# Attention and feed-forward kernel: query tiles 2 and 3 turned by VectorE and moved by DMA instead of turned by TensorE

## The chip, the core and the metric

The kernel runs on 1 of the cores of one Trainium2 chip. The metric is the time of one execution on the device in microseconds (us). Engines: TensorE (PE, matmuls), VectorE (DVE), ScalarE (ACT), GpSimd (POOL), and SyncE (SP), which here only issues DMA transfers.

## The reference

The input x has 4 batches of 1024 tokens of 128 numbers, all float32. Attention with 16 heads of 64 comes first, then a layer norm, a small feed-forward part and a second layer norm:

```python
s = einsum('bhid,bhjd->bhij', q * 64**-0.5, k)
gm = max(s, axis=-1, keepdims=True)            # over all columns, masked or not
p = where(triu(ones, 1), 0.0, exp(s - gm))     # causal
out = einsum('bhij,bhjd->bhid', p, v) / (sum(p, -1) + 1e-8)
x = layernorm(x + out @ Wo + bo)
r = sigmoid(mix(x, mu_r) @ W_r.T); k = square(relu(mix(x, mu_k) @ W_k.T))
x = layernorm(x + r * (k @ W_v.T))             # mix: mu * x + (1 - mu) * the token before
```

## The kernel before

Two heads are worked on at a time: a pair. There are 8 pairs in each of 4 batches, so 32 pairs (p) one after the other, and the feed-forward part follows behind them. The 1024 queries of a pair are 8 tiles of 128; one step (t) of a pair makes the scores of tile t for both heads (a = 0, 1). The program of each engine is written out as a loop over p and t, so the order on each engine is the order in the code; semaphores tie the engines together.

One tile goes this way. TensorE writes 128x1024 scores into one of 3 score buffers (`ps_s`, line 758). VectorE moves them, scaled and with their running minimum, into one of 4 slots of `tile` in SBUF (`evacuate`, line 585); a slot comes free two steps later, when its tile is turned. GpSimd masks the 128x128 block on the diagonal (line 340), ScalarE takes the exp of the (t+1)*128 columns that count and sums them (line 434). The values matmul needs this probability tile with keys on the partitions, so it is turned, into `pt`:

- Tiles 0 to 3 are turned on TensorE (`turn_tile`, line 771: one 128x128 transpose for each block of keys, t+1 of them for each head), into one of the 2 shared banks `ps_x`, and ScalarE copies them to `pt` (`take_turned`, lines 472 and 479). They are turned one step later than their scores.
- Tiles 4 to 7 are turned in 32x32 blocks by VectorE (line 596) into a staging buffer. When both tiles of a unit (unit u is tiles 2u and 2u+1) are turned, SyncE moves the blocks to their partitions with 16 transfers (`move`, line 290), each from 32 partitions to 32 partitions. There are 32 such transfers a pair.

The values matmuls (`values`, line 808) come in three parts: part 0 (units 0 and 1) in step 7 of the same pair, part 1 (unit 2) in step 5 of the next pair, part 2 (unit 3) in step 6 of the next pair. What they give goes through ScalarE (`take_values`, line 457) to `ot`, is scaled by 1/sum on GpSimd (`norm`, line 347, with `rb`, which two DMA transfers from ScalarE's queue spread), is projected by TensorE (`project_out`, line 819, half 0 in step 4), and is added to `y`. Between these stand the projections of the next pair: three matmuls for each half of q and k (line 694, steps 0 to 3), which ScalarE takes and GpSimd splits into a high and a low part, and the value projections (line 703, steps 0 and 1).

The two shared banks `ps_x` go round in the order of their users (`users_of_banks`); a user waits until the one before it in its bank has been copied out (`drained`).

## Time and profile before

| | |
|---|---|
| time, median of 3 runs | 1148.97 us (1145.62 to 1149.92) |
| profiled execution: time, span | 1145.66 us, 1143.9 us |
| TensorE busy | 1042.7 us, 91% |
| VectorE busy | 924.4 us, 81% |
| ScalarE busy | 735.7 us, 64% |
| GpSimd busy | 565.8 us, 49% |
| mean granted TensorE clock | 0.982 of full |
| transfers stage to pt | 1024 issues, all on SyncE's queue |

Times are of one profiled execution. A matmul row of the timeline merges neighbours of one form, so its start is what to read, not its length: the next row starts when TensorE goes on. Busy shares are means over the whole span; what ends a wait is read from the timeline.

### The profile page before, as it was taken

What the parts mean: (1) busy time and instruction counts of PE and PEld (TensorE: products, weight loads), DVE (VectorE), ACT (ScalarE), POOL (GpSimd) and SP (SyncE); (2) the same over time, 40 slices, a digit from 0 to 9 for tenths busy, and PEclk for the clock granted to TensorE, in tenths of its full rate; (3) what the DMA queues carried; (4) which work ended last, traced back from release to release, by engine and by line L of the source; (5) the groups of instructions that cost most, each with busy time, mean ns of one, the idle gap of its engine ahead of it and who ended that gap; (6) DMA issues with size and microseconds to landing.
All of it is one profiled execution on the core that took longest, in us unless ns stands there. A gap on an engine that the chain in (4) does not pass through costs nothing.

```text
span 1143.9 us, 21976 instructions
## 1 busy us (share of the span) xinstructions
PE 1042.7 (91%) x7411; PEld 675.9 (59%) x7411; DVE 924.4 (81%) x1588; ACT 735.7 (64%) x1666; POOL 565.8 (49%) x904
## 2 busy tenths in 40 slices
...
GB/s 154 82 131 125 129 129 146 149 135 126 120 111 128 133 139 148 143 119 117 129 125 125 134 148 148 126 127 114 125 125 131 144 148 141 120 114 136 83 38 37
DMA packets 172497, 142.44 MB, mean 125 GB/s; under 512 B 26849, under 2 KB 167905, under 8 KB 172385
## 3 DMA queue, kind: packets, MB, share of 16 engines
...
q14 instruction: 54, 0.43, 0.1%
...
## 4 chain that ended last, share of the span: by engine, by line
PE 45%; DVE 23%; issue 12%; POOL 10%; DMA 5%; ACT 2%; SPq 2%; ACTq 1%; DVEq 0%; POOLq 0%
PE ps_s L758 18%; PE ps_x L808 17%; DVE tile L585 12%; DVE stage L596 6%; POOL ot L347 4%; DMA rb<-recips 4%; PE ps_x L819 4%; POOL tile L340 2%; POOL qs L334 2%; PE ps_x L694 2%; PE ps_x L771 2%; SPq L290 2%; PE ps_x L703 1%; POOL qs L332 1%; DVE stats L611 1%
## 5 line engine op out<-in xcount | busy, mean ns | idle before, releaser
L585 DVE TENSOR_SCALAR_CACHE_REDUCE tile<-ps_s 128x1024 f32<-128x1024 f32 x512 | 604.5, 1217 | 175.3 <-PE ps_s L758 173.9
L434 ACT ACTIVATE tile<-tile,neg_max 128x640 f32<-128x640 f32 (+7 forms) x512 | 394.3, 773 | 178.9 <-POOL tile L340 175.2
L758 PE MATMUL ps_s<-ks,qs 64*128 64x512 f32 x3072 | 426.0, 409 | 9.1 <-DVE tile L585 7.0
L340 POOL TENSOR_SCALAR_AFFINE_SELECT tile<-tile 128x128 f32<-128x128 f32 x512 | 148.2, 292 | 426.2 <-DVE tile L585 424.6
L758 PEld LDWEIGHTS ps_s<-ks,qs 64*128 64x128 f32 x3072 | 270.2, 185 | 116.1 <-DVE tile L585 39.3
L808 PE MATMUL ps_x<-pt,vs 128*64 128x256 f32 (+1 forms) x2560 | 270.4, 362 | 2.8 <-DMA pt<-stage 2.8
L596 DVE STREAM_TRANSPOSE stage<-tile 128x640 f32<-128x640 f32 (+3 forms) x256 | 249.7, 1014 | 0.0
L808 PEld LDWEIGHTS ps_x<-pt,vs 128*64 128x64 f32 x2560 | 173.6, 137 | 111.2 <-issue 37.7
L694 PE MATMUL ps_x<-xs,ws 128*128 128x512 f32 x381 | 121.7, 428 | 15.2 <-ACT vs L447 14.5
L347 POOL TENSOR_TENSOR ot<-ot,rb 128x512 f32<-128x512 f32 x64 | 99.2, 1550 | 66.3 <-ACT ot L457 56.1
L771 PE MATMUL ps_x<-ident,tile 128*128 128x128 f32 x640 | 113.8, 284 | 11.9 <-ACT tile L434 10.4
L771 PEld LDWEIGHTS ps_x<-ident,tile 128*128 128x128 f32 x640 | 69.8, 140 | 83.8 <-issue 58.0
L479 ACT ACTIVATE pt<-ps_x 128x256 f32<-128x256 f32 (+2 forms) x192 | 90.6, 489 | 31.7 <-PE ps_x L771 29.0
L441 ACT ACTIVATE x1t<-ps_x 128x512 f32<-128x512 f32 x124 | 74.5, 600 | 55.8 <-PE ps_x L694 34.5
L434 ACT ACTIVATION_READ_ACCUMULATOR tile<-tile,neg_max 128x1 f32 x512 | 97.2, 190 | 0.0
L819 PE MATMUL ps_x<-ot,wos 128*128 128x512 f32 x128 | 73.0, 652 | 25.6 <-POOL ot L347 25.6
L354 POOL TENSOR_TENSOR y<-y,ot 128x512 f32<-128x512 f32 x64 | 82.9, 1295 | 7.1 <-ACT ot L462 7.1
L694 PEld LDWEIGHTS ps_x<-xs,ws 128*128 128x128 f32 x381 | 62.8, 191 | 34.1 <-ACT vs L447 21.9
L334 POOL TENSOR_TENSOR qs<-x1t,qs 128x512 fp32r<-128x512 f32 x62 | 79.5, 1282 | 5.3
L334 POOL TENSOR_TENSOR ks<-x1t,ks 128x512 fp32r<-128x512 f32 x62 | 78.9, 1273 | 5.1
L462 ACT ACTIVATE ot<-ps_x 128x512 f32<-128x512 f32 x64 | 38.2, 597 | 48.3 <-PE ps_x L819 48.3
L703 PEld LDWEIGHTS ps_x<-ws,xs 128*128 128x128 f32 x384 | 49.8, 188 | 28.7 <-ACT ot L457 16.2
...
## 6 DMA issues: line engine op xcount, KB each, us to landing
pt<-stage SPq DMA_DIRECT2D x512, 128.0 KB, 4.6
pt<-stage SPq DMA_DIRECT2D x512, 96.0 KB, 2.2
...
```

Of the source, the lines that this page charges most:

```text
L334: pool.tensor_tensor(lo, full[n % 2], hi.bitcast(F32), ALU.subtract).then_inc(s_qklo, 1)
L340: pool.affine_select(out=block_of, in_=block_of, compare_op=ALU.is_ge, fill=fill, base=0, pattern=[[-1, P]], channel_multiplier=1).then_in ...
L347: pool.tensor_tensor(cols, cols, rb[:, :].rearrange("p (i t) -> p t i", t=TILES)[:, 4 * c:4 * c + 4, :], ALU.mult).then_inc(s_norm, 1)
L434: act.activation(cols, cols, ACT.Exp, bias=neg_max[:, at:at + 1], scale=-1.0, accum_out=sums[:, p % 2, a, t:t + 1]).then_inc(s_exp, 1)
L479: act.activation(place, cols, ACT.Copy).then_inc(s_pt, 1)
L585: dve.tensor_scalar(tile[:, at, :], ps_s[scores_at(p, t, a)][:, :], -SCALE, None, ALU.mult, ALU.min, accum_out=neg_max[:, at:at + 1]).then ...
L596: dve.transpose(stage_unit(u)[:, 2 * a + t % 2, :, 0:32 * (t + 1)], tile[:, slot_of(p, t, a), 0:(t + 1) * P].rearrange("p (j b k) -> p b j ...
L694: ins = mm(bank, ws[:, "qk".index(what), wh, r * P:(r + 1) * P], xs[:, b % XSLOTS, xh, c * HALF:(c + 1) * HALF], start=(m == 0), stop=(m = ...
L758: ins = mm(ps_s[scores_at(p, t, a)][:, c * HALF:(c + 1) * HALF], qs[rows, p % 2, qh, t * P:(t + 1) * P], ks[rows, p % 2, kh, c * HALF:(c + ...
L771: ins = turn(ps_x[BANK[unit]][:, at:at + P], tile[:, slot_of(p, t, a), j * P:(j + 1) * P], ident[:, :])
L808: ins = mm(bank[a * DH:(a + 1) * DH, cols + second * P:cols + 2 * P], vs[:, p // 2 % 2, j, p % 2, a * DH:(a + 1) * DH], moving, start=(j = ...
L819: mm(ps_x[BANK[unit]][:, :], wos[:, p % PAIRS, :], ot[:, c * HALF:(c + 1) * HALF], start=True, stop=True).then_inc(s_out, 1)
```

## The change

Tiles 2 and 3 go the way of tiles 4 to 7. `BLOCKWISE` is now tiles 2 to 7; TensorE turns tiles 0 and 1 only. There are three units to move, 48 transfers a pair, in the order unit 3 of the pair before, unit 1, unit 2. `pt` and the staging buffers have a new layout, in which the two tiles of a unit and both heads lie side by side without gaps, so that each transfer has 32 runs (one for each partition, of 448, 704 or 960 numbers for units 1, 2, 3) where it had 128 (of 192 or 256 numbers). The memsets of the gaps are gone. Unit 1 is read by the values matmuls of the same pair, in step 7.

The orders change too: on VectorE the second turn of tile 7 stands behind the first evacuation of step 1; on TensorE and ScalarE the turned tile comes ahead of the value projection in step 1; ScalarE takes out half 0 in step 5, not 4. The value tiles 4 to 7 have one place instead of two. Two more buffers for the halves of q and k keep ScalarE and GpSimd apart.

```diff
--- before.py
+++ after.py
@@ -27,14 +27,16 @@
 UNITS = TILES // 2
-UNIT_COLS = [(2 * u + 2) * 32 for u in range(UNITS)]
-UNIT_AT = [16 * sum(UNIT_COLS[:u]) for u in range(UNITS)]
+HEAD_COLS = [(4 * u + 3) * 32 for u in range(UNITS)]
+UNIT_COLS = [2 * cols for cols in HEAD_COLS]
+UNIT_AT = [4 * sum(UNIT_COLS[:u]) for u in range(UNITS)]
+PT_COLS = 4 * sum(UNIT_COLS)
 MOVED = 16 * 16
-BLOCKWISE = range(TILES // 2, TILES)
-
-TURNED_IN = {0: ((0, 1),), 1: ((0, 1),), 2: ((0,), (1,)), 3: ((0,), (1,))}
-COPIES = {(0, 0): 1, (1, 0): 3, (2, 0): 4, (2, 1): 5, (3, 0): 6, (3, 1): 7}
-ALL_COPIES = 7
+BLOCKWISE = range(2, TILES)
+
+TURNED_IN = {0: ((0, 1),), 1: ((0, 1),)}
+COPIES = {(0, 0): 1, (1, 0): 3}
+ALL_COPIES = 3
@@ -43,7 +45,7 @@
 V_AT = {0: 0, 1: 1}
-TURN_AT = {1: 0, 2: 1, 3: 2, 4: 3}
+TURN_AT = {1: 0, 2: 1}
 X_AT = 1
@@ -58,6 +60,10 @@
     return 2 * ((TILES * p + t) % (RING // 2)) + a
+
+
+def v_place(i, j):
+    return i % 2 * 4 + j if j < 4 else 4 + j
...
@@ -129,19 +135,20 @@
         ks = sb("ks", [P, 2, 2, N], F32R)
-        vs = sb("vs", [P, 2, TILES, 2, P])
+        vs = sb("vs", [P, TILES + 4, 2, P])
         tile = sb("tile", [P, RING, N])
         recips = sb("recips_sb", [P, 2, 2, TILES])
-        stage = [sb(f"stage{n}", [P, 16 * UNIT_COLS[2 + n]]) for n in range(2)]
-        pt = sb("pt", [P, 16 * sum(UNIT_COLS)])
+        stage = [sb(f"stage{n}", [P, 4 * UNIT_COLS[1 + n]]) for n in range(3)]
+        pt = sb("pt", [P, PT_COLS])
         ot = sb("ot", [P, N])
         x1t = sb("x1t", [P, 1 + N])
-        full = [x1t[:, 1:1 + HALF], x1t[:, 1 + HALF:1 + N]]
+        full2 = sb("full2", [P, HALF])
+        full = [x1t[:, 1:1 + HALF], x1t[:, 1 + HALF:1 + N], full2[:, :], x1t[:, 1:1 + HALF]]
         bo_col = sb("bo_col", [P, 1])
@@ -160,14 +167,18 @@
         def stage_unit(u):
-            return stage[u - 2][:, :].rearrange("p (x b c) -> p x b c", x=4, b=4)
+            return stage[u - 1][:, :].rearrange("p (b c) -> p b c", b=4)
         def pt_unit(u):
-            return pt[:, UNIT_AT[u]:UNIT_AT[u] + 16 * UNIT_COLS[u]].rearrange("p (x a c) -> p x a c", x=4, a=4)
-
-
-
-        idle = pt[:, UNIT_AT[3]:UNIT_AT[3] + 4 * N]
+            return pt[:, UNIT_AT[u]:UNIT_AT[u] + 4 * UNIT_COLS[u]].rearrange("p (a c) -> p a c", a=4)
+
+        def place_of(t, a):
+            at = a * HEAD_COLS[t // 2] + t % 2 * 32 * t
+            return slice(at, at + 32 * (t + 1))
+
+
+
+        idle = pt[:, PT_COLS - 4 * N:PT_COLS]
         x_raw = [idle[:, 0:N]] + [y[:, b * N:(b + 1) * N] for b in range(1, B)]
...
@@ -278,21 +288,23 @@
                 if p == 0 and u == 2:
-                    sp.wait_ge(s_gaps, 2)
                     sp.wait_ge(f_wt, 1)
                 at_least(sp, s_pv, 3 * (p - 1) + u)
-                sp.wait_ge(s_turned, 8 * p + 4 * (u - 2) + 4)
+                sp.wait_ge(s_turned, 12 * p + 4 * u)
                 for a in range(4):
                     for b in range(4):
-                        sp.dma_start(pt_unit(u)[32 * b:32 * b + 32, :, a, :], stage_unit(u)[32 * a:32 * a + 32, :, b, :]
-                                     ).then_inc(s_moved[u - 2], 16)
-
-            for p in range(ALL_PAIRS):
-                move(p, 2)
-                move(p, 3)
+                        sp.dma_start(pt_unit(u)[32 * b:32 * b + 32, a, :], stage_unit(u)[32 * a:32 * a + 32, b, :]
+                                     ).then_inc(s_moved[u - 1], 16)
+
+            for p in range(ALL_PAIRS + 1):
+                if p > 0:
+                    move(p - 1, 3)
+                if p < ALL_PAIRS:
+                    move(p, 1)
+                    move(p, 2)
@@ -310,10 +322,6 @@
-            for n in range(2):
-                pool.memset(stage[n][:, :], 0.0).then_inc(s_gaps, 1)
-
-
             pool.wait_ge(s_wraw, 48)
@@ -329,9 +337,9 @@
                 pool.wait_ge(s_full, done + 1)
-                pool.tensor_copy(hi, full[n % 2]).then_inc(s_qkhi, 1)
+                pool.tensor_copy(hi, full[n]).then_inc(s_qkhi, 1)
                 pool.wait_ge(s_qkhi, done + 1)
-                pool.tensor_tensor(lo, full[n % 2], hi.bitcast(F32), ALU.subtract).then_inc(s_qklo, 1)
+                pool.tensor_tensor(lo, full[n], hi.bitcast(F32), ALU.subtract).then_inc(s_qklo, 1)
@@ -437,14 +445,16 @@
                 act.wait_ge(s_proj, done + 1)
-                at_least(act, s_qklo, done - 1)
-                act.activation(full[n % 2], ps_x[BANK["qk", p, n]][:, :], ACT.Copy).then_inc(s_full, 1)
+
+                at_least(act, s_qklo, done - {0: 0, 1: 3, 2: 3, 3: 2}[n])
+                act.activation(full[n], ps_x[BANK["qk", p, n]][:, :], ACT.Copy).then_inc(s_full, 1)
-                at_least(act, s_pv, 6 * (i - 1))
-                act.activation(vs[:, i % 2, 2 * n:2 * n + 2, :, :],
+                at_least(act, s_pv, 6 * (i - 1) if n < 2 else 6 * i)
+                at = v_place(i, 2 * n)
+                act.activation(vs[:, at:at + 2, :, :],
                                ps_x[BANK["v", i, n]][:, :].rearrange("p (t e c) -> p t e c", t=2, e=2), ACT.Copy
...
@@ -500,26 +510,27 @@
                         take_out(p - 2, 1)
+                    if t in TURN_AT and p < ALL_PAIRS:
+                        take_turned(p, TURN_AT[t], 0)
                     if t in V_AT and p < ALL_PAIRS:
                         take_v(p // 2, 2 * (p % 2) + V_AT[t])
-                    if t in TURN_AT and p < ALL_PAIRS:
-                        take_turned(p, TURN_AT[t], 0)
                     if t in QK_AT and p + 1 < ALL_PAIRS:
                         take_qk(p + 1, QK_AT[t])
-                    if t == OUT0_AT and 0 < p:
+                    if t == OUT0_AT + 1 and 0 < p:
                         take_out(p - 1, 0)
-                    if t in TURN_AT and p < ALL_PAIRS and len(TURNED_IN[TURN_AT[t]]) > 1:
-                        take_turned(p, TURN_AT[t], 1)
                     if t == X_AT and p < ALL_PAIRS:
                             take_x(b, c)
+                    if t == 1 and p > 0:
+                        spread_recips(p - 1)
                     if p < ALL_PAIRS:
                         exp_of(p, t, 0)
+                    if t in TURN_AT and p < ALL_PAIRS and len(TURNED_IN[TURN_AT[t]]) > 1:
+                        take_turned(p, TURN_AT[t], 1)
+                    if p < ALL_PAIRS:
                         exp_of(p, t, 1)
                         column_recips(p - 1)
-                    if t == 1 and p > 0:
-                        spread_recips(p - 1)
                     if t == 5 and p > 0:
@@ -577,9 +588,9 @@
                 if u in BLOCKWISE:
-                    at_least(dve, s_turned, 8 * q + 2 * (u - 4) + a + 1)
+                    at_least(dve, s_turned, 12 * q + 2 * (u - 2) + a + 1)
                 else:
-                    dve.wait_ge(s_quad, 8 * q + 2 * u + a + 1)
+                    dve.wait_ge(s_quad, 4 * q + 2 * u + a + 1)
                 dve.wait_ge(s_scores, SLOTS * p + 2 * t + a + 1)
@@ -589,11 +600,9 @@
-                    at_least(dve, s_moved[u - 2], MOVED * p)
-                if p == 0 and t == 4 and a == 0:
-                    dve.wait_ge(s_gaps, 2)
+                    at_least(dve, s_moved[u - 1], MOVED * p)
                 dve.wait_ge(s_exp, SLOTS * p + 2 * t + a + 1)
-                dve.transpose(stage_unit(u)[:, 2 * a + t % 2, :, 0:32 * (t + 1)],
+                dve.transpose(stage_unit(u)[:, :, place_of(t, a)],
                               tile[:, slot_of(p, t, a), 0:(t + 1) * P].rearrange("p (j b k) -> p b j k", b=4, k=32)
@@ -637,6 +646,9 @@
                         evacuate(p, t, 0)
+                    if t == 1 and p > 0:
+                        turn_tile(p - 1, TILES - 1, 1)
+                    if p < ALL_PAIRS:
                         evacuate(p, t, 1)
@@ -646,7 +658,8 @@
                         turn_tile(q, u, 0)
-                        turn_tile(q, u, 1)
+                        if u < TILES - 1:
+                            turn_tile(q, u, 1)
                     if p == ALL_PAIRS and t == SUMS_AT:
@@ -795,18 +808,22 @@
                     pe.wait_ge(s_pt, ALL_COPIES * (p + 1))
-                else:
-                    pe.wait_ge(s_moved[k - 1], MOVED * (p + 1))
                 for u in units:
+                    if u > 0:
+                        pe.wait_ge(s_moved[u - 1], MOVED * (p + 1))
                     cols = (u % 2) * 2 * P
                     for j in range(final + 1):
-
-                        second = j == final
                         for a in range(2):
-                            moving = pt_unit(u)[:, 2 * a + second:2 * a + 2, :, 32 * j:32 * j + 32]
-                            ins = mm(bank[a * DH:(a + 1) * DH, cols + second * P:cols + 2 * P],
-                                     vs[:, p // 2 % 2, j, p % 2, a * DH:(a + 1) * DH], moving,
+                            at = a * HEAD_COLS[u]
+                            if j < final:
+                                both = pt_unit(u)[:, :, at:at + 2 * 32 * final].rearrange("p a (t c) -> p t a c", t=2)
+                                moving = both[:, :, :, 32 * j:32 * j + 32]
+                            else:
+
+                                moving = pt_unit(u)[:, :, at + 32 * (final + j):at + 32 * (final + j) + 32]
+                            ins = mm(bank[a * DH:(a + 1) * DH, cols + (j == final) * P:cols + 2 * P],
+                                     vs[:, v_place(p // 2, j), p % 2, a * DH:(a + 1) * DH], moving,
                                      start=(j == 0), stop=(j == final))
@@ -839,16 +856,16 @@
                         project_out(p - 2, 1)
+                    if t in TURN_AT and p < ALL_PAIRS:
+                        turn_tile(p, TURN_AT[t], 0)
                     if t in V_AT and p < ALL_PAIRS:
                         v_of(p // 2, 2 * (p % 2) + V_AT[t])
-                    if t in TURN_AT and p < ALL_PAIRS:
-                        turn_tile(p, TURN_AT[t], 0)
                     if t in QK_AT and p + 1 < ALL_PAIRS:
                         qk_of(p + 1, QK_AT[t])
+                    if t in TURN_AT and p < ALL_PAIRS and len(TURNED_IN[TURN_AT[t]]) > 1:
+                        turn_tile(p, TURN_AT[t], 1)
                     if t == OUT0_AT and 0 < p:
                         project_out(p - 1, 0)
-                    if t in TURN_AT and p < ALL_PAIRS and len(TURNED_IN[TURN_AT[t]]) > 1:
-                        turn_tile(p, TURN_AT[t], 1)
                     if t == X_AT and p < ALL_PAIRS:
```

VectorE, from the evacuations of step 7 of one pair to those of step 5 of the next, as it was (`[waits ...]` names semaphores; 128x4x160 is a turned tile of 640 columns, 128x4x224 one of 896):

```order
L585 TENSOR_SCALAR tile,neg_max<-ps_s 128x1024 [waits s_scores,s_turned] x2
L602 TENSOR_SCALAR sums_eps<-sums 128x16 [waits s_exp]
L606 RECIPROCAL recips_sb<-sums_eps 128x16 [waits s_eps,s_rdram]
L596 STREAM_TRANSPOSE stage<-tile 128x1024 [waits s_exp] x2
L585 TENSOR_SCALAR tile,neg_max<-ps_s 128x1024 [waits s_scores,s_turned] x2
L585 TENSOR_SCALAR tile,neg_max<-ps_s 128x1024 [waits s_scores,s_quad] x8
L596 STREAM_TRANSPOSE stage<-tile 128x4x160 [waits s_exp,s_moved0]
L596 STREAM_TRANSPOSE stage<-tile 128x4x160 [waits s_exp]
L585 TENSOR_SCALAR tile,neg_max<-ps_s 128x1024 [waits s_scores,s_turned] x2
```

And as it is now (128x4x96 is tile 2 with 384 columns, 128x4x128 tile 3 with 512):

```order
L596 TENSOR_SCALAR tile,neg_max<-ps_s 128x1024 [waits s_scores,s_turned] x2
L611 TENSOR_SCALAR sums_eps<-sums 128x16 [waits s_exp]
L615 RECIPROCAL recips_sb<-sums_eps 128x16 [waits s_eps,s_rdram]
L605 STREAM_TRANSPOSE stage<-tile 128x4x256 [waits s_exp]
L596 TENSOR_SCALAR tile,neg_max<-ps_s 128x1024 [waits s_scores,s_turned]
L605 STREAM_TRANSPOSE stage<-tile 128x4x256 [waits s_exp]
L596 TENSOR_SCALAR tile,neg_max<-ps_s 128x1024 [waits s_scores,s_turned]
L596 TENSOR_SCALAR tile,neg_max<-ps_s 128x1024 [waits s_scores,s_quad] x4
L605 STREAM_TRANSPOSE stage<-tile 128x4x96 [waits s_exp,s_moved0]
L605 STREAM_TRANSPOSE stage<-tile 128x4x96 [waits s_exp]
L596 TENSOR_SCALAR tile,neg_max<-ps_s 128x1024 [waits s_scores,s_turned] x2
L605 STREAM_TRANSPOSE stage<-tile 128x4x128 [waits s_exp] x2
```

Four turned tiles stand where there were none, two behind the evacuations of step 3 and two behind those of step 4, and the second turn of tile 7 stands between the two evacuations of step 1.

TensorE, steps 3 and 4 behind the scores of step 3, before (L771 is a transpose, L694 a projection of q or k, L819 the projection of the output, L758 the scores):

```order
L771 MATMUL ps_x<-ident,tile 128x128 [waits s_exp,s_pt]
L771 MATMUL ps_x<-ident,tile 128x128 x2
L694 MATMUL ps_x<-xs,ws 128x512 [waits s_full]
L694 MATMUL ps_x<-xs,ws 128x512 x2
L771 MATMUL ps_x<-ident,tile 128x128 [waits s_exp,s_pt]
L771 MATMUL ps_x<-ident,tile 128x128 x2
L758 MATMUL ps_s<-ks,qs 128x512 [waits s_evac]
L758 MATMUL ps_s<-ks,qs 128x512 x11
L771 MATMUL ps_x<-ident,tile 128x128 [waits s_exp,s_full]
L771 MATMUL ps_x<-ident,tile 128x128 x3
L819 MATMUL ps_x<-ot,wos 128x512 [waits s_pt,s_norm]
L771 MATMUL ps_x<-ident,tile 128x128 [waits s_exp,s_pt]
```

Now (L771 is here the scores, L707 the projection, L836 the output's):

```order
L771 MATMUL ps_s<-ks,qs 128x512 [waits s_evac]
L771 MATMUL ps_s<-ks,qs 128x512 x11
L707 MATMUL ps_x<-xs,ws 128x512 [waits s_pt]
L707 MATMUL ps_x<-xs,ws 128x512 x2
L771 MATMUL ps_s<-ks,qs 128x512 [waits s_evac]
L771 MATMUL ps_s<-ks,qs 128x512 x11
L836 MATMUL ps_x<-ot,wos 128x512 [waits s_full,s_norm]
L771 MATMUL ps_s<-ks,qs 128x512 [waits s_evac]
L771 MATMUL ps_s<-ks,qs 128x512 x11
```

Of steps 3 and 4, one projection and one output projection are left beside the scores.

TensorE, step 7 before: its scores, the values matmuls (L808), and the scores of the next pair:

```order
L758 MATMUL ps_s<-ks,qs 128x512 [waits s_evac]
L758 MATMUL ps_s<-ks,qs 128x512 x11
L808 MATMUL ps_x<-pt,vs 64x256 [waits s_pt,s_vs,s_ot]
L808 MATMUL ps_x<-pt,vs 64x256
L808 MATMUL ps_x<-pt,vs 64x128 x2
L808 MATMUL ps_x<-pt,vs 64x256 x6
L808 MATMUL ps_x<-pt,vs 64x128 x2
L758 MATMUL ps_s<-ks,qs 128x512 [waits s_evac,s_qklo]
L758 MATMUL ps_s<-ks,qs 128x512 x11
```

The same place now (L825 the values, L771 the scores):

```order
L771 MATMUL ps_s<-ks,qs 128x512 [waits s_evac]
L771 MATMUL ps_s<-ks,qs 128x512 x11
L825 MATMUL ps_x<-pt,vs 64x256 [waits s_pt,s_vs,s_ot]
L825 MATMUL ps_x<-pt,vs 64x256
L825 MATMUL ps_x<-pt,vs 64x128 x2
L825 MATMUL ps_x<-pt,vs 64x256 [waits s_moved0]
L825 MATMUL ps_x<-pt,vs 64x256 x5
L825 MATMUL ps_x<-pt,vs 64x128 x2
L771 MATMUL ps_s<-ks,qs 128x512 [waits s_evac,s_qklo]
L771 MATMUL ps_s<-ks,qs 128x512 x11
```

Unit 0 is read first, then the matmul that waits for `s_moved0`, unit 1, and behind it the scores. Before, this part waited for `s_pt`, `s_vs` and `s_ot` only. SyncE's queue held, for each pair, 16 transfers of 32x4x192 and 16 of 32x4x256; it now holds 16 of 32x960 (unit 3 of the pair before), 16 of 32x448 (unit 1) and 16 of 32x704 (unit 2).


## Rows read from the trace of the kernel before

**Rows 1.** The page: busy time by engine, and the chain that ended last.

```profile
PE 1042.7 (91%) x7411; PEld 675.9 (59%) x7411; DVE 924.4 (81%) x1588; ACT 735.7 (64%) x1666; POOL 565.8 (49%) x904
PE 45%; DVE 23%; issue 12%; POOL 10%; DMA 5%; ACT 2%; SPq 2%; ACTq 1%; DVEq 0%; POOLq 0%
```

**Rows 2.** Timeline of TensorE, one pair: start, length, engine, line, tiles, count.

```profile
497.85 1.67 PE L758 MATMUL ps_s<-ks,qs 64*128 64x512 f32 x12
...
502.23 1.65 PE L758 MATMUL ps_s<-ks,qs 64*128 64x512 f32 x12
...
506.37 1.65 PE L758 MATMUL ps_s<-ks,qs 64*128 64x512 f32 x12
...
509.45 1.67 PE L758 MATMUL ps_s<-ks,qs 64*128 64x512 f32 x12
...
512.72 1.66 PE L758 MATMUL ps_s<-ks,qs 64*128 64x512 f32 x12
...
515.56 1.12 PE L819 MATMUL ps_x<-ot,wos 128*128 128x512 f32 x2 [0.20 <-POOL ot L347]
...
517.05 1.66 PE L758 MATMUL ps_s<-ks,qs 64*128 64x512 f32 x12
...
527.73 2.38 PE L808 MATMUL ps_x<-pt,vs 128*64 128x256 f32 x24
530.04 1.67 PE L758 MATMUL ps_s<-ks,qs 64*128 64x512 f32 x12
```

**Rows 3.** Timeline of VectorE in the same pair.

```profile
500.05 1.18 DVE L585 TENSOR_SCALAR_CACHE_REDUCE tile<-ps_s 128x1024 f32<-128x1024 f32 x1
...
504.99 1.19 DVE L585 TENSOR_SCALAR_CACHE_REDUCE tile<-ps_s 128x1024 f32<-128x1024 f32 x1
...
511.25 1.22 DVE L585 TENSOR_SCALAR_CACHE_REDUCE tile<-ps_s 128x1024 f32<-128x1024 f32 x1 [0.73 <-PE ps_s L758]
...
514.51 1.22 DVE L585 TENSOR_SCALAR_CACHE_REDUCE tile<-ps_s 128x1024 f32<-128x1024 f32 x1 [0.88 <-PE ps_s L758]
...
521.13 1.56 DVE L596 STREAM_TRANSPOSE stage<-tile 128x640 f32<-128x640 f32 x2
...
525.25 1.83 DVE L596 STREAM_TRANSPOSE stage<-tile 128x768 f32<-128x768 f32 x2
```

**Rows 4.** Timelines of ScalarE (exp of tile 1, head 1) and GpSimd (norm of half 0).

```profile
507.73 0.51 ACT L434 ACTIVATE tile<-tile,neg_max 128x256 f32<-128x256 f32 x1 [0.17 <-POOL tile L340]
...
508.15 0.19 ACT L434 ACTIVATION_READ_ACCUMULATOR tile<-tile,neg_max 128x1 f32 x1
...
513.96 1.54 POOL L347 TENSOR_TENSOR ot<-ot,rb 128x512 f32<-128x512 f32 x1
```

**Rows 5.** Issues from stage to pt: all, three timeline pieces, and landing (window 527 to 534).

```profile
L290 SPq DMA_DIRECT2D pt<-stage x1024: 585/607/2074, 41.0 to 1067.1; - x171
...
527.16 0.58 SPq L290 DMA_DIRECT2D pt<-stage  x1
527.78 1.25 SPq L290 DMA_DIRECT2D pt<-stage  x2
528.43 1.26 SPq L290 DMA_DIRECT2D pt<-stage  x2
...
DMA to landing us min/median/max: 2.2/2.2/3.5
```

**Rows 6.** Issues of other transfers: ns min/median/max, and two starts.

```profile
L264 SPq DMA_DIRECT2D pt<-in_L_attn_x x2: 433/465/497, 0.7 to 1.2; - x2
...
L271 SPq DMA_DIRECT2D pt<-in_L_ffn_W_r x1: 432/432/432, 3.5 to 3.5; - x1
...
3.48 0.43 SPq L271 DMA_DIRECT2D pt<-in_L_ffn_W_r  x1
3.96 0.43 SPq L271 DMA_DIRECT2D pt<-in_L_ffn_W_k  x1
...
L492 ACTq DMA_DIRECT2D rb<-recips x64: 452/562/845, 53.3 to 1054.7; - x64
```

13 lines of the change are left out of this document (6 added, 7 removed).

## Prediction

> **What bounds the kernel now.** I read the page first. TensorE is busy for 91% of the span, VectorE for 81%, and the chain that ended last lies 45% on TensorE, 23% on VectorE and 10% on GpSimd [rows 1]. An average over a program made of 32 equal stretches tells little about which wait ends last, so I went on to the timeline of one pair of heads in the middle (p is the pair, t the step). I call S(t) the start of the scores of step t on TensorE and D(t) the start of the first evacuation of that step on VectorE. The reader is to see that S(0) is at 497.85 and the next S(0) at 530.04: a pair takes 32.19 us. The steps are S(1) 502.23, S(2) 506.37, S(3) 509.45, S(4) 512.72, S(5) 517.05 [rows 2]. TensorE has hardly a gap in the pair, so the pair is its work plus a few waits in steps 3 and 4, where VectorE stands idle 0.73 and 0.88 us for scores [rows 3].
>
> Then I looked at what only hides behind TensorE. On VectorE: D(0) 500.05, D(1) 504.99, D(3) 511.25, D(4) 514.51; two evacuations take 2.29 us start to start (evacuations for one step are 128x1024 each, 1.14 apart), two turned tiles of 640 columns 1.56, two of 768 columns 1.83 [rows 3]. On GpSimd the norm of out half 0 starts at 513.96, 2.71 after D(3), and TensorE's project_out starts right behind its end [rows 2, 4]. On the queue of SyncE: 16 transfers of a unit start 0.62 to 0.65 us after each other (527.16, 527.78, 528.43), each issue takes 0.61 us in the median over all 1024 of them, and in this unit a transfer lands 2.2 us after its issue [rows 5]. So a unit needs 15 x 0.655 + 2.2 = 12.0 us from its last turned tile until TensorE may read it. Today nobody waits for that, since units 2 and 3 are read five and six steps into the next pair.
>
> **What the change removes.** Tiles 2 and 3 are no longer turned by TensorE: 6 + 8 = 14 of 20 transposes of a pair, and 4 of 6 copies of ScalarE, are gone. Steps 0 to 2 keep theirs. What is the gain? In step 3 TensorE would need its scores and one projection only, but the ring of three score buffers lets S(4) start only after the first evacuation of step 3 has ended. From the rows, D(3) is 1.80 after S(3), and an evacuation with its read takes about 1.23, plus about 0.07 to start: S(4) = S(3) + 3.1 instead of 3.27. In step 4 the next thing late is the norm: project_out started 515.56, that is S(3) + 6.11, and took 0.96 until the turn behind it began, which is now S(5). So S(5) = S(3) + 7.07 where it was 7.60 (517.05 - 509.45) [rows 2 to 4]. The gain that is left is 0.53 us a pair, not the two microseconds of TensorE work that were taken away. Steps 5 to 7 (517.05 to 530.04) hold the same matmuls as before; VectorE has 2.29 + 1.56, 2.29 + 1.83 and about 2.29 + 2.10 there, less than the 12.99 of TensorE. I leave them.
>
> **Steps 0 to 2.** The second turn of tile 7 moves from step 0 behind the first evacuation of step 1. D(1) gets earlier by it, from S(1) + 2.76 to about S(1) + 1.8, but the second evacuation of step 1 stands behind the turn (1.15), so exp of tile 1, head 1 (507.73, its read until 508.34, which is S(1) + 6.1 [rows 4]) ends at 1.8 + 4.5 = 6.3 after S(1). It was hardly waited for before and will cost TensorE some 0.4 in step 2; the new order in step 1 (turn, value projection, key projection) saves about 0.4 of waiting for a bank. I cost the two at nothing together, with -0.5 and +0.5 as ends, and keep S(3) - S(0) = 11.60 [rows 2]. The value tiles in one place wait for reads that ended steps earlier (s_pv, step 6 of the pair before the write): nothing. The memsets of the gaps at the start go; the loads cover them: nothing. The later take of out half 0 on ScalarE stands where ScalarE has lost two copies: nothing, and 0.6 if that cover is gone.
>
> **What it adds on VectorE.** By the rows, two turned tiles cost 0.27 less for each 128 columns: 2 x 384 columns 1.02, 2 x 512 columns 1.29, together 2.3 a pair [rows 3]. Tile 2 is turned after the evacuations of step 3, tile 3 after those of step 4. With S(3) = 11.60 and D(3) = 13.40, D(4) = 13.40 + 2.29 + 1.02 = 16.7 (before: 514.51 - 497.85 = 16.66, so nothing is late for it), and tile 3 is turned at 16.7 + 2.29 + 1.29 = 20.3 after S(0).
>
> **What it adds on the queue, and the sum.** Unit 1 (tiles 2 and 3) is now moved by 16 transfers, and it is read in the same pair, in step 7, by the second part of values(p, 0). This is the new wait, and the term that decides. The queue is free by then (unit 3 of the pair before starts after tile 7, head 1, at about 8.5, and its 16 issues end at 19.0). So: 20.3 + 0.08 (turned tile at 527.08, issue at 527.16) + 15 x 0.655 = 30.2 for the last issue, + 2.2 = 32.4 landed, + 0.05 to start. Behind it stand the matmuls of unit 1, 1792 of the 2560 columns of the 2.31 us from 527.73 to 530.04, so 1.62, and only then the scores of the next pair: S(0)' = 34.05. Queued behind the waiting matmul is everything TensorE has, and VectorE and GpSimd run dry a step later. Without the wait TensorE would start the next pair at 32.19 - 0.53 = 31.66, so the stall is 34.05 - 31.66 = 2.4 us, and what the pair loses against today is 34.05 - 32.19 = 1.86. Times 32 pairs is 59.5. The profiled execution took 1145.66 us (span 1143.9, 1.8 around it), which gives 1205; the median of the runs shown is 3 us higher, and I don't add that.
>
> **The one unknown size** is the distance between issues for the new shape: 32 partitions with one run of 448, 704 or 960 numbers instead of four runs each. With d for it the pair is 24.25 + 15 d, and it meets 32.19 at d = 0.53. Upper end: the rows of today's moves, 0.65. Lower end: loads from DRAM with one run for each partition start 0.48 apart (3.48, 3.96) and take 0.43 [rows 6], which gives 31.45, earlier than the 31.66 that the norm chain sets, so 31.66 it is. I take the upper end, for this reason: the load of x has four runs for each of 128 partitions and still takes 0.43 to 0.50, the loads of weights have one run and take 0.43 [rows 6]. Runs do not show as a price there. The transfer of rb, 64 partitions with one run, takes 0.56 in the median. What sets the moves apart from all of these is that both ends lie in SBUF and that they have 32 partitions, and both stay. And the two units today, 768 and 1024 bytes a run, start equally far apart, so bytes don't set it either.
>
> The Trainium skill (DMA: Bandwidth & Descriptors, Issuing engines are not separate DMA queues) says that the time on the sequencer to start a DMA "is usually small relative to the DMA itself". The trace disagrees for these: 16 issues take 10.4 us and one transfer lands in 2.2 [rows 5]. By that rule the unit would be there in a few microseconds, nobody would wait, and the time would be that of the first rival.
>
> **Rivals.** (1) *The issue gets short with one run, and the unit is in time.* Then the pair is 31.66, 0.53 less, x 32 = 17, so 1128; with the 0.5 of steps 0 to 2 down to 1115 at best. For it: 0.43 of the loads, and that the first issue of a unit took 0.58, so 0.6 is not made by a full queue. Against it: the x loads above. This is the side on which the kernel gets faster; it decides from d = 0.507 down (0.5% of 1146 is 5.7 us, 0.18 a pair; that much is about what a measurement can tell from no change). (2) *In between*, d from 0.507 to 0.54: the stall eats what the transposes gave, 1140 to 1152. Nothing in the rows lies there but the 0.50 of some loads and the 0.56 of rb. (3) *The queue is full.* 48 issues a pair at 0.655 are 31.4 us, 92% of 34.05; single issues today take up to 2.1 us [rows 5], and one or two such in a pair push unit 3, then unit 1. One in each unit-1 block adds about 0.5 to 1 a pair: 1220 to 1237. (4) *The change does only half*: if TensorE waits in step 7, its clock could be granted lower. Its idle share would be 9% and it had the full clock with waits of 1 us in the middle stretches, so I give it no chance of its own.
>
> **How the numbers follow.** Forecast (d near 0.65, stall in each pair) 0.52; rival 3 0.08; rival 1 0.28; rival 2 0.12. Slower by over 0.5%: 0.52 + 0.08 + a small part of rival 2 = 0.61; faster 0.28; within 0.5% 0.11. The forecast's own range is 1188 to 1220 (d 0.62 to 0.66, steps 0 to 2 off by 0.3). The cases of both signs hold much, so the range for 8 in 10 reaches down to rival 1's 1124 and up to 1222.
>
> **What would show it.** In the profile after: issues of the moves at 0.6 us, 0.65 apart; a wait of TensorE in the values line, released by the DMA into pt, 32 times, some 2.0 to 3.0 us each, and none like it at units 2 and 3; VectorE's turned tiles of 384 and 512 columns at about 0.5 and 0.65 us; S(5) - S(3) near 7.1 us. I am wrong if the issues are under 0.5 us, or if TensorE meets no wait for pt and the pair is under 32 us; and wrong about the gain if S(5) - S(3) has shrunk by 1.5 or more.

## The result and the profile after

The changed kernel takes 1207.7 us (median of 4 runs, 1207.6 to 1211.5) where the kernel before takes 1147.8 us (4 runs): 1.053 times as long, 95% interval 1.050 to 1.056. The profiled execution took 1207.73 us.

The page after: busy time and chain as in [rows 1], and the groups of the values matmul and of the issues. The columns of a group are busy time, mean ns of one, idle time before it and what ended most of that.

```profile
PE 998.9 (83%) x6963; PEld 634.3 (53%) x6963; DVE 998.0 (83%) x1716; ACT 688.1 (57%) x1538; POOL 558.7 (46%) x902
PE 29%; SPq 26%; DVE 20%; issue 14%; DMA 6%; ACT 3%; POOL 2%; ACTq 0%; DVEq 0%; POOLq 0%
SPq L299 26%; PE ps_s L771 12%; DVE tile L596 11%; DMA pt<-stage 5%; DVE stage L605 5%; PE ps_x L825 5%; PE ps_x L707 4%; PE ps_x L836 3%; PE ps_x L716 2%; ACT tile L442 2%; PE ps_x L784 1%; POOL tile L348 1%; DVE stats L620 1%; DMA pt<-in_L_attn_Wkv 1%; DVE pt L642 1%
L825 PE MATMUL ps_x<-pt,vs 128*64 128x256 f32 (+1 forms) x2560 | 282.4, 368 | 65.1 <-DMA pt<-stage 65.1
pt<-stage SPq DMA_DIRECT2D x512, 120.0 KB, 3.6
pt<-stage SPq DMA_DIRECT2D x512, 88.0 KB, 2.1
pt<-stage SPq DMA_DIRECT2D x512, 56.0 KB, 2.0
```

TensorE's share fell from 91% to 83%, but the chain now lies 26% on the queue of SyncE, which had 2% before. The values matmul waited 65.1 us for the DMA into `pt`, where it had waited 2.8.

The waits after, TensorE and its weight loads: who waited for whom, us in total, times, longest.

```profile
PEld ps_x L825 <- DMA pt<-stage: 71.3, 32, 3.1
PEld ps_x L836 <- POOL ot L355: 65.6, 33, 8.6
PE ps_x L825 <- DMA pt<-stage: 65.1, 33, 2.9
PE ps_x L836 <- POOL ot L355: 51.8, 33, 8.3
PE ps_x L784 <- ACT tile L442: 27.5, 57, 1.4
```

There are 33 such waits in the 32 pairs, 2.0 us each in the mean. The timeline of TensorE for one pair, to be held against [rows 2]:

```profile
524.91 1.74 PE L825 MATMUL ps_x<-pt,vs 128*64 128x256 f32 x16 [2.29 <-DMA pt<-stage]
526.58 1.66 PE L771 MATMUL ps_s<-ks,qs 64*128 64x512 f32 x12
...
530.93 1.66 PE L771 MATMUL ps_s<-ks,qs 64*128 64x512 f32 x12
...
534.39 1.66 PE L771 MATMUL ps_s<-ks,qs 64*128 64x512 f32 x12
536.46 0.41 PE L784 MATMUL ps_x<-ident,tile 128*128 128x128 f32 x2 [0.41 <-ACT tile L442]
537.42 0.44 PE L784 MATMUL ps_x<-ident,tile 128*128 128x128 f32 x2 [0.55 <-ACT tile L442]
...
538.49 1.67 PE L771 MATMUL ps_s<-ks,qs 64*128 64x512 f32 x12
...
541.57 1.66 PE L771 MATMUL ps_s<-ks,qs 64*128 64x512 f32 x12 [0.52 <-DVE tile L596]
544.57 1.13 PE L836 MATMUL ps_x<-ot,wos 128*128 128x512 f32 x2 [1.33 <-POOL ot L355]
545.62 1.66 PE L771 MATMUL ps_s<-ks,qs 64*128 64x512 f32 x12
...
556.29 0.87 PE L825 MATMUL ps_x<-pt,vs 128*64 128x256 f32 x8
558.61 1.73 PE L825 MATMUL ps_x<-pt,vs 128*64 128x256 f32 x16 [1.44 <-DMA pt<-stage]
560.27 1.66 PE L771 MATMUL ps_s<-ks,qs 64*128 64x512 f32 x12
```

The pair takes 560.27 - 526.58 = 33.69 us where it took 32.19. It is one of the shorter ones: in the mean of the pairs 2 to 29 step 7 lasts 6.16 us, and here 560.27 - 554.71 = 5.56. The first row is the same wait at the end of the pair before, 2.29 us. Unit 0 is read at 556.29, and unit 1 comes at 558.61. VectorE and SyncE of the same pair, the turned tiles 2 and 3 (beside [rows 3]) and the issues of unit 1 (beside [rows 5]):

```profile
542.58 1.03 DVE L605 STREAM_TRANSPOSE stage<-tile 128x384 f32<-128x384 f32 x2
...
545.80 1.30 DVE L605 STREAM_TRANSPOSE stage<-tile 128x512 f32<-128x512 f32 x2
...
L299 SPq DMA_DIRECT2D pt<-stage x1536: 507/591/1846, 32.9 to 1128.0; - x192
...
547.72 1.86 SPq L299 DMA_DIRECT2D pt<-stage  x3
...
549.62 1.86 SPq L299 DMA_DIRECT2D pt<-stage  x3
```

Tile 3 is turned at 547.10 and the first issue starts at 547.17. Three issues after 547.72 the next starts at 549.62, so 0.633 us lie between two. The last of the 16 starts at 556.59, 9.42 us after the first; it lands 2.0 us later and the matmul starts at 558.61. Nothing but the queue lies on that stretch.

### The profile page after: what moved, and what is told of

The parts are those of the page before. It is cut to its first block, busy times and chain, and to the rows that moved or that the text cites. A ratio compares the mean times of both kernels' runs of the same rounds, so it can differ in the third digit from the quotient of the medians.

```text
span 1205.6 us, 21400 instructions
## 1 busy us (share of the span) xinstructions
PE 998.9 (83%) x6963; PEld 634.3 (53%) x6963; DVE 998.0 (83%) x1716; ACT 688.1 (57%) x1538; POOL 558.7 (46%) x902
## 4 chain that ended last, share of the span: by engine, by line
PE 29%; SPq 26%; DVE 20%; issue 14%; DMA 6%; ACT 3%; POOL 2%; ACTq 0%; DVEq 0%; POOLq 0%
SPq L299 26%; PE ps_s L771 12%; DVE tile L596 11%; DMA pt<-stage 5%; DVE stage L605 5%; PE ps_x L825 5%; PE ps_x L707 4%; PE ps_x L836 3%; PE ps_x L716 2%; ACT tile L442 2%; PE ps_x L784 1%; POOL tile L348 1%; DVE stats L620 1%; DMA pt<-in_L_attn_Wkv 1%; DVE pt L642 1%
## 5 line engine op out<-in xcount | busy, mean ns | idle before, releaser
L771 PE MATMUL ps_s<-ks,qs 64*128 64x512 f32 x3072 | 429.2, 411 | 25.5 <-DVE tile L596 23.7
L771 PEld LDWEIGHTS ps_s<-ks,qs 64*128 64x128 f32 x3072 | 272.3, 186 | 160.4 <-issue 59.2
L825 PE MATMUL ps_x<-pt,vs 128*64 128x256 f32 (+1 forms) x2560 | 282.4, 368 | 65.1 <-DMA pt<-stage 65.1
L605 DVE STREAM_TRANSPOSE stage<-tile 128x768 f32<-128x768 f32 (+5 forms) x384 | 328.2, 887 | 0.0
L825 PEld LDWEIGHTS ps_x<-pt,vs 128*64 128x64 f32 x2560 | 175.0, 138 | 183.2 <-DMA pt<-stage 71.3
L707 PE MATMUL ps_x<-xs,ws 128*128 128x512 f32 x381 | 122.1, 429 | 0.9 <-DVE xs L571 0.4
L836 PE MATMUL ps_x<-ot,wos 128*128 128x512 f32 x128 | 73.9, 660 | 51.8 <-POOL ot L355 51.8
L450 ACT ACTIVATE x1t<-ps_x 128x512 f32<-128x512 f32 x93 | 55.8, 600 | 38.1 <-PE ps_x L707 37.8
L707 PEld LDWEIGHTS ps_x<-xs,ws 128*128 128x128 f32 x381 | 62.7, 190 | 25.0 <-issue 12.7
L716 PE MATMUL ps_x<-ws,xs 128*128 128x256 f32 x384 | 70.7, 320 | 0.0
L784 PE MATMUL ps_x<-ident,tile 128*128 128x128 f32 x192 | 41.3, 296 | 27.5 <-ACT tile L442 27.5
L836 PEld LDWEIGHTS ps_x<-ot,wos 128*128 128x128 f32 x128 | 19.4, 191 | 77.1 <-POOL ot L355 65.6
L467 ACT ACTIVATE ot<-ps_x 128x256 f32<-128x256 f32 (+1 forms) x96 | 42.2, 440 | 23.2 <-PE ps_x L825 23.1
```

The lines of the kernel that those rows point to most:

```text
L605: dve.transpose(stage_unit(u)[:, :, place_of(t, a)], tile[:, slot_of(p, t, a), 0:(t + 1) * P].rearrange("p (j b k) -> p b j k", b=4, k=32) ...
L707: ins = mm(bank, ws[:, "qk".index(what), wh, r * P:(r + 1) * P], xs[:, b % XSLOTS, xh, c * HALF:(c + 1) * HALF], start=(m == 0), stop=(m = ...
L716: ins = mm(bank[:, 2 * t * P:2 * (t + 1) * P], xs[:, b % XSLOTS, xh, at], ws[:, 2, wh, r * P:(r + 2) * P], start=(m == 0), stop=(m == 2))
L771: ins = mm(ps_s[scores_at(p, t, a)][:, c * HALF:(c + 1) * HALF], qs[rows, p % 2, qh, t * P:(t + 1) * P], ks[rows, p % 2, kh, c * HALF:(c + ...
L825: ins = mm(bank[a * DH:(a + 1) * DH, cols + (j == final) * P:cols + 2 * P], vs[:, v_place(p // 2, j), p % 2, a * DH:(a + 1) * DH], moving, ...
L836: mm(ps_x[BANK[unit]][:, :], wos[:, p % PAIRS, :], ot[:, c * HALF:(c + 1) * HALF], start=True, stop=True).then_inc(s_out, 1)
```

## Experiments

All times are medians beside runs of the kernel before on the same chip; the ratio to it has its 95% interval.

**Tiles 2 and 3 back on TensorE**, everything else of the change kept.

```diff
-BLOCKWISE = range(2, TILES)
+BLOCKWISE = range(4, TILES)
-TURN_AT = {1: 0, 2: 1}
+TURN_AT = {1: 0, 2: 1, 3: 2, 4: 3}
...
-                    move(p, 1)
```

The lines left out set the counts of semaphores to match.

> Tiles 2 and 3 go back to TensorE and ScalarE; layout, orders, value places and buffers of the change stay, and SyncE has 32 transfers a pair, each with 32 runs. Theory (the whole loss is the wait for unit 1 in step 7): no wait for pt in step 7, 1142 to 1152, like the kernel before. Rival (the new layout or the new orders cost something of their own, for instance exp of tile 1, head 1 that ends later): 1160 to 1185. If the orders alone are a gain: below 1140.

Measured: 1159.1 us, ratio 1.0104 (1.0079 to 1.0128). Between theory and rival: the wait for `pt` is gone and most of the loss with it, and about 11 us are left. Of the two TensorE rows below the first is in step 5 (it waits for the bank that a copy of tile 3 holds), the second in step 2 (exp of tile 1). The ScalarE rows show why the copy is late.

```profile
527.49 2.60 PE L824 MATMUL ps_x<-pt,vs 128*64 128x256 f32 x24 [0.69 <-ACT pt L488]
...
549.74 0.44 PE L783 MATMUL ps_x<-ident,tile 128*128 128x128 f32 x2 [0.60 <-ACT tile L441]
...
526.03 0.83 ACT L441 ACTIVATE tile<-tile,neg_max 128x640 f32<-128x640 f32 x1 [2.06 <-POOL tile L347]
...
526.86 0.57 ACT L488 ACTIVATE pt<-ps_x 128x512 f32<-128x512 f32 x1
```

In the mean of the pairs 2 to 29 step 5 lasts 4.87 us where it lasted 4.12 before, which is 24 us in 32 pairs and more than the whole loss. It comes from one order of the change on ScalarE: the copy of head 1 stands behind exp of head 0, and here that exp waits for its mask. The changed kernel has no tile that is copied in two parts, so this wait can't arise in it, and the 11 us are no price of its orders. Steps 3 and 4 are 0.36 us shorter than before. Steps 0 to 2 are what the two kernels share: 11.93 us in the mean where the kernel before has 11.74, and 11.91 in the changed one.

**Half of the transfers of unit 1 left out**, and **all of them with a quarter of the bytes.**

```diff
-                for a in range(4):
+                for a in range(2 if u == 1 else 4):
...
```

```diff
+                        n = UNIT_COLS[u] // 4 if u == 1 else UNIT_COLS[u]
-                        sp.dma_start(pt_unit(u)[32 * b:32 * b + 32, a, :], ...
+                        sp.dma_start(pt_unit(u)[32 * b:32 * b + 32, a, 0:n], ...
```

> The changed kernel with 8 of the 16 transfers of unit 1 left out (two of four source blocks are not moved, so part of the probabilities of tiles 2 and 3 is missing from the values). Theory: the unit lands 8 x 0.634 = 5.1 us earlier, the wait of 2.0 us a pair in step 7 is gone, and 65 us with it: 1143, at least 1130 to 1152. Rival 1 (the turned tiles that VectorE has more bound the pair): the wait goes over to VectorE and the time stays over 1190. If the gain of the transposes was more than the 0.53 us a pair of the prediction, the time is under 1125.

> The changed kernel with all 16 transfers of unit 1, but each moves only the first quarter of its columns (448 bytes a run for 1792; the rest of unit 1 is left out of the computation). Theory (the number of issues sets the wait, not bytes): issues stay 0.63 apart, landing is at most 0.2 us shorter, 1200 to 1209. Rival (the transfers themselves are slow, bytes set the wait): the wait falls by half or more, 1145 to 1175.

Measured: half the count 1131.5 us, ratio 0.9862 (0.9839 to 0.9884). A quarter of the bytes 1203.2 us, ratio 1.0478 (1.0450 to 1.0506). Of the second, the wait and the time to landing:

```profile
PE ps_x L830 <- DMA pt<-stage: 60.7, 33, 4.1
...
pt<-stage SPq DMA_DIRECT2D x512, 14.0 KB, 1.8
```

Three quarters of the bytes are worth 0.2 us of landing time (1.8 for 2.0) and 4.5 us in all; half of the issues are worth 76 us. So the wait is made by the number of issues on one queue. Half the count lands below the 1143 that taking away the 65 us would give, because the row of the wait counts too little. Its step 7 shows what the same matmuls take without the wait:

```profile
553.01 2.38 PE L829 MATMUL ps_x<-pt,vs 128*64 128x256 f32 x24
555.33 0.96 PE L775 MATMUL ps_s<-ks,qs 64*128 64x512 f32 x6
```

They take 2.32 us from start to start, and 560.27 - 556.29 = 3.98 after the change, so the counted wait of 1.44 costs 1.66. In the mean of the pairs 2 to 29 step 7 lasts 6.16 us after the change and 3.90 here: the stall is 2.26 us a pair, 72 us in 32. And VectorE with its added turns is no bound: without the wait the kernel is faster than before.

**Part 0 of the values matmuls later**, behind the scores and projections of step 0 of the next pair.

```diff
...
-                    if t == 7 and p < ALL_PAIRS:
-                        values(p, 0, (0, 1))
...
+                    if t == 0 and p > 0:
+                        values(p - 1, 0, (0, 1))
```

> The changed kernel with part 0 of the values matmuls (units 0 and 1) moved from the end of step 7 to the end of step 0 of the next pair, behind its scores and projections; everything is computed. Theory: unit 1 is then wanted some 5 us later, nobody waits for it, and VectorE gets its scores meanwhile: 1130 to 1146. Rival 1: the queue of SyncE with 48 issues a pair becomes the bound and the wait turns up at unit 2 or 3: 1170 to 1200. Rival 2: the late norm of half 0 on GpSimd holds up the output projection in step 4, which takes the gain back: 1150 to 1170.

Measured: 1181.3 us, ratio 1.0293 (1.0271 to 1.0314). The wait for unit 1 is gone but for 4.7 us in all, as the theory had it, but neither the theory's time nor the place that a rival named came out. TensorE in step 0, its first row and the next scores:

```profile
545.63 1.65 PE L771 MATMUL ps_s<-ks,qs 64*128 64x512 f32 x12 [1.51 <-DVE tile L596]
547.21 1.13 PE L836 MATMUL ps_x<-ot,wos 128*128 128x512 f32 x2
547.77 1.28 PE L716 MATMUL ps_x<-ws,xs 128*128 128x256 f32 x6
549.03 0.97 PE L707 MATMUL ps_x<-xs,ws 128*128 128x512 f32 x3
549.92 2.38 PE L825 MATMUL ps_x<-pt,vs 128*64 128x256 f32 x24
552.24 1.65 PE L771 MATMUL ps_s<-ks,qs 64*128 64x512 f32 x12
```

Step 7 has nothing left to fill the time in which VectorE turns tile 6, so TensorE waits 1.51 us for a score buffer; and step 0 grows to 6.6 us (545.63 to 552.24), in which VectorE runs dry (1.56 us before it). With three score buffers the work must stay level from step to step. My expectation had counted the wait and not what the matmuls were covering.

**Four of the 16 transfers of unit 1 from ScalarE's queue**, in step 6, and then the orders of steps 0 and 1 one by one on top of it.

```diff
-                for a in range(4):
+                for a in range(3 if u == 1 else 4):
...
+            def move_rest(p):
+                act.wait_ge(s_turned, 12 * p + 4)
+                for b in range(4):
+                    act.dma_start(pt_unit(1)[32 * b:32 * b + 32, 3, :], stage_unit(1)[96:128, b, :]
+                                  ).then_inc(s_moved[0], 16)
...
+                    if t == 6 and p < ALL_PAIRS:
+                        move_rest(p)
```

> The changed kernel, everything computed, with 4 of the 16 transfers of unit 1 issued from ScalarE's queue in step 6 and 12 from SyncE's. Theory (the wait in step 7 is the serial issue of 16 transfers): the last issue on SyncE is 2.5 us earlier, at 20.5 + 0.1 + 11 x 0.634 = 27.6 after S(0), landed at 29.6, and TensorE wants it at 30.5, so the wait is gone and the time is that of the half-count kernel plus what the issues cost ScalarE: 1130 to 1142, faster than the kernel before. Rival (a full queue: the transfers share the same engines, so another queue doesn't help): over 1180. Rival 2 (the 4 issues hold up the exp of steps 6 and 7): 1150 to 1175.

> As e6_four_on_act, with both turns of tile 7 back in step 0 on VectorE. Theory (the second evacuation of step 1 behind a turn delays exp of tile 1, head 1, and TensorE waits 0.55 us for it in step 2): 0.2 to 0.5 us a pair less, 6 to 15 us below e6_four_on_act. Rival (the wait for exp of head 0, 0.41 us, and VectorE's longer step 0 decide instead): no difference, or slower by up to 10 us.

> As e6_four_on_act, with the two issues of rb back behind both exps of step 1 on ScalarE. Theory (ScalarE's queue is held 1.1 us by them and exp of tile 1, head 0 starts 1.1 us after its mask; TensorE waits 0.41 us for it): 0.1 to 0.4 us a pair less, 3 to 13 us below e6_four_on_act. Rival (rb comes later then, and the norm of half 0, which TensorE waits for 1.3 us in step 4, comes later with it): slower by 5 to 30 us.

> As e6_four_on_act, with both of these orders as they were before the change. Theory: the waits for the two exps in step 2 are gone, S(3) - S(0) falls from 11.91 to about 11.2, 15 to 22 us below e6_four_on_act. Rival (the norm of half 0 sets step 4 and absorbs it, since rb lands later): within 5 us of e6_four_on_act.

The edits of the last three are the lines of the change on `turn_tile(p - 1, TILES - 1, 1)` and on `spread_recips(p - 1)`, undone.

| kernel | us | ratio to before (95%) |
|---|---|---|
| 4 issues on ScalarE | 1138.9 | 0.9929 (0.9911 to 0.9947) |
| and tile 7 turned in step 0 | 1132.4 | 0.9867 (0.9848 to 0.9886) |
| and rb spread behind the exps | 1153.6 | 1.0065 (1.0036 to 1.0094) |
| both | 1134.5 | 0.9863 (0.9823 to 0.9902) |

The first is the fix that says it most plainly: the same 48 transfers, all results computed, 69 us less, only by a second queue. Of the wait for `pt` this is left:

```profile
PE ps_x L833 <- DMA pt<-stage: 6.3, 9, 2.1
```

Tile 7 in step 0 gains 6.5 us as expected: the waits for exp of tile 1 (0.41 and 0.55 us after the change) are not in its timeline; a wait of 0.55 us for a score buffer, ahead of the scores of step 2, stands there instead.

The spread of rb behind the exps was expected to gain and lost 15 us (its rival). In step 2 its TensorE waits once and longer for the second exp, in place of the two waits:

```profile
546.78 0.44 PE L792 MATMUL ps_x<-ident,tile 128*128 128x128 f32 x2 [1.03 <-ACT tile L442]
```

This is not the place of the loss: S(3) - S(0) is 11.90 us in the mean where it is 11.92 with the two issues ahead. The loss is in steps 4 and 5 of a few pairs. The later rb lands 16.0 us after S(0) in the median of the pairs (13.7 with the issues ahead), and GpSimd could start the norm of half 0 at 16.4. So where a landing is slow, the norm waits for it, and TensorE for the norm. Pair 5 on GpSimd and TensorE, and one stretch of it with the granted clock (the number behind the five busy times):

```profile
192.55 1.52 POOL L355 TENSOR_TENSOR ot<-ot,rb 128x512 f32<-128x512 f32 x1 [1.75 <-DMA rb<-recips]
...
194.12 2.08 PE L844 MATMUL ps_x<-ot,wos 128*128 128x512 f32 x2 [3.12 <-POOL ot L355]
196.12 2.93 PE L779 MATMUL ps_s<-ks,qs 64*128 64x512 f32 x12
...
196.00:198.00 2.00, 2.00 (x11) 1.49 (x10) 0.00 (x0) 1.76 (x5) 1.92 (x4) 0.50 0.36 92
```

A norm that is 1.75 us late costs this pair 4.6 us, because the granted clock of TensorE is 0.50 behind the wait of 3.12 us: the 12 score matmuls take 2.93 us for 1.65. The pairs 5, 8, 20 and 30 have this, and together they are 10.6 of the 12.8 us between the two profiled executions.

With both orders back the expectation (15 to 22 us below the first kernel) failed: 4.5 us, which is its rival. S(3) - S(0) falls to 11.59 in the mean, not 11.2, and the late rb costs in step 4 (4.21 us in the mean for 4.05). Against tile 7 alone (1132 and 1134) no difference can be told; the five runs of it spread from 1126 to 1137.

**The kernel before with the order of tile 7 only**, and **unit 1 with four runs for each partition.**

> The kernel before with one order of the change only: the second turn of tile 7 on VectorE between the two evacuations of step 1. Theory (exp of tile 1, head 1 ends about 0.5 us too late for TensorE in step 2, while in the kernel before TensorE sits out 0.47 us in step 1 anyway): 0.2 to 0.5 us a pair, 6 to 16 us slower than before, 1153 to 1163. Rival (the order is free, as the prediction had it): within 3 us of before.

```diff
+                    if t == 1 and p > 0:
+                        turn_tile(p - 1, TILES - 1, 1)
...
```

Measured: 1153.7 us, ratio 1.0039 (1.0024 to 1.0053). The order costs 4 us in the old kernel too. That is less than the 6 to 16 expected and more than the 3 that the rival allowed, and the interval excludes no change. In the profiled executions S(3) - S(0) grows by 0.25 us in the mean, all of it in step 2.

> The changed kernel, each of the 16 transfers of unit 1 with four runs of 448 bytes in each of 32 partitions instead of one of 1792 (same bytes; they land at other columns, so the values of tiles 2 and 3 are not the reference's). Theory (runs are a small part of an issue; in the trace before four runs were 0.655 apart, after the change one run is 0.634): 15 x 0.021 = 0.3 us a pair, 8 to 12 us slower than the changed kernel, 1214 to 1222. Rival (runs are no part, the 0.02 has another cause): within 3 us of 1207. Rival 2 (128 short runs take longer on the transfer engines and land later): over 1230.

```diff
...
+                            dst = pt_unit(1)[32 * b:32 * b + 32, :, a * n:(a + 1) * n]
+                            src = stage_unit(1)[32 * a:32 * a + 32, :, b * n:(b + 1) * n]
```

Measured: 1227.1 us, ratio 1.0661 (1.0616 to 1.0705; single runs 1218 to 1231), 19 us more than one run for each partition, twice what was expected. The last five issues of unit 1 of one pair on SyncE's queue, with the row of all issues and the wait:

```profile
L304 SPq DMA_DIRECT2D pt<-stage x1536: 507/593/2021, 32.9 to 1151.3; - x192
...
534.44 4.11 SPq L304 DMA_DIRECT2D pt<-stage  x5
...
PE ps_x L829 <- DMA pt<-stage: 80.7, 33, 4.5
```

In unit 1 two issues start 0.644 apart in the median (0.633 with one run), which is 0.2 us of the 0.6 us a pair. One issue, at 535.73, takes 1.53 us instead of 0.60; such single long issues are in every kernel here, and four runs make no more of them: 17 over 0.9 us in unit 1, and 19 with one run. From the first issue of unit 1 to the last it takes 10.25 us in the mean (9.89 with one run), and the last one lands 0.1 us later; step 7 grows by 0.5 us. The rest is TensorE's clock: behind waits of 2.6 to 3.6 us it was granted at half in 8 stretches between S(0) of pair 1 and of pair 31 (3 with one run), and step 0 is 0.2 us longer in the mean.

**The next wait taken away: the norm of half 0 between the two masks of step 3**, on top of the kernel with 4 issues on ScalarE and tile 7 in step 0.

```diff
                         mask(p, t, 0)
+                    if t == 3 and 0 < p <= ALL_PAIRS:
+                        norm(p - 1, 0)
+                    if p < ALL_PAIRS:
                         mask(p, t, 1)
```

> As e7_tile7_back, everything computed, with the norm of half 0 on GpSimd between the two masks of step 3 instead of behind both. Theory (TensorE waits 1.35 us in step 4 for this norm, and behind it the next limit is VectorE's evacuation of step 4, 0.6 to 0.7 us earlier than now): 0.5 to 0.7 us a pair less, 16 to 22 us below e7_tile7_back, 1109 to 1118. Rival (the later mask of step 3, head 1 delays exp, and with it tile 3 and the issue of unit 1): the wait for pt in step 7 comes back and the time stays within 5 us of 1132.

Measured: 1114.6 us, ratio 0.9701 (0.9670 to 0.9732), as the theory had it, everything computed: 3% faster than the kernel before and 7.7% faster than the changed one. Its step 3 to 5 on TensorE:

```profile
529.32 1.65 PE L776 MATMUL ps_s<-ks,qs 64*128 64x512 f32 x12
532.38 1.66 PE L776 MATMUL ps_s<-ks,qs 64*128 64x512 f32 x12 [0.52 <-DVE tile L605]
534.47 1.13 PE L841 MATMUL ps_x<-ot,wos 128*128 128x512 f32 x2 [0.43 <-POOL ot L355]
535.60 1.66 PE L776 MATMUL ps_s<-ks,qs 64*128 64x512 f32 x12
...
547.67 1.73 PE L830 MATMUL ps_x<-pt,vs 128*64 128x256 f32 x16 [0.51 <-DMA pt<-stage]
```

S(5) - S(3) is 6.28 where it was 7.13, and the wait for unit 1 begins to come back in this pair (17.6 us in all), since a shorter pair asks for it earlier.

## Why the prediction was right, step by step

The mechanism, its place and its price came out: 1205 predicted, 1207.7 measured. In the mean of the pairs 2 to 29 the three terms are: steps 0 to 2 +0.17 us (predicted 0), steps 3 and 4 -0.60 (predicted -0.53), the stall in step 7 +2.26 (predicted +2.39); together +1.83 where the sum had +1.86. That it comes so close is in part luck, as the items below show: two errors of the queue's term cancel.

- *The issue distance stays that of transfers within SBUF.* Predicted 0.655 from today's moves against 0.48 from loads; measured 0.633, an issue 0.591 against 0.607. Runs are a small part of it. This choice carried the whole prediction, and the half-count and second-queue kernels show that it was the right term.
- *The path to unit 1.* Tile 3 turned at 20.3 after S(0), measured 547.10 - 526.58 = 20.52; last issue at 30.2, measured 30.0; landed 32.4, measured 32.0; the matmuls of unit 1 1.62, measured 1.66; pair 34.05, in this pair 33.69. The mean over the kernel is (1205.6 - 1143.9)/32 = 1.93 us more a pair against 1.86 predicted. The pair shown has 16 issues without a long one; the pair before it waited 2.29 us instead of 1.44. The sum had 15 x 0.655 = 9.83 from the first issue to the last; without a long issue it is 9.42, and in the mean over the 32 units 1 it is 9.89, with 19 issues over 0.9 us in them. So the long issues, the third rival's addition (0.5 to 1 us a pair), came in at 0.47, and they make up what the shorter distance saves.
- *The stall* was to be 2.4 us a pair; the counted wait is 2.0 (65.1 us in 32), and what it costs, by the length of step 7, is 2.26.
- *The gain left from 14 transposes.* S(5) - S(3) was to be 7.07, and it is 545.62 - 538.49 = 7.13. Step 3 is limited by VectorE's evacuation (the 0.52 us) and step 4 by the norm (1.33 us), as worked out. With the stall removed and tile 7 in its old place the pair was to be 31.66, and that kernel is 1132.4 where the sum gave 1128. The kernel with the norm moved shows that this was the next limit.
- *Steps 0 to 2 at nothing* was a little too low: S(3) - S(0) is 11.91 and not the 11.60 of the pair that was read, within the end of 0.5 that was kept. Against the mean of the kernel before (11.74) it is 0.17 us a pair: step 1 lost 0.66 and step 2 gained 0.81. The cause for the second exp was named (the turn ahead of the second evacuation), that for the first was not seen: the two issues of rb stand ahead of exp of tile 1, head 0 on ScalarE and hold its queue 1.1 us. Moving them away gains nothing in these steps, as the kernel with rb spread behind the exps shows.
- *The clock at no chance* (rival 4) was not quite right. TensorE was granted half its clock in 3 short stretches between S(0) of pair 1 and of pair 31, each behind a wait of 2.1 to 2.4 us in step 7; before the change there was none. They cost some 5 us of the 60, an estimate from the steps beside them. One of them:

```profile
1004.00:1008.00 4.00, 3.40 (x18) 1.93 (x20) 2.22 (x4) 1.94 (x5) 0.29 (x1) 0.57 0.58 139
```

- *A slip in the rivals*: with 24.25 + 15 d, a gain of 0.18 us a pair needs d = 0.517, not 0.507, so rival 2 starts there. It changes nothing here.
- *The memsets, value places and buffers at nothing*: no wait names them.
- The rule of the Trainium skill (DMA: Bandwidth & Descriptors, Issuing engines are not separate DMA queues) that the time to start a DMA is usually small beside the DMA itself misleads here: one issue takes 0.59 us and lands in 2.0, but the 16 of a unit start one after the other, 9.4 us from first to last. The same sentence says that starting DMAs from several engines saves that time and nothing else, and the kernel with 4 issues on ScalarE agrees: 69 us.
